# Image tokens: the second layernorm's scaling on GpSimd, the last image group in two parts

## The reference, cut to what matters

```
x = img.reshape(B, C, h, P, w, P)                       # 32 images, 14 x 14 patches of 16 x 16 x 3
x = jnp.transpose(x, (0, 2, 4, 3, 5, 1)).reshape(B, h * w, P * P * C)
x = _layernorm(x, ln1_g, ln1_b)                         # over 768 values
x = jnp.einsum('bnp,pd->bnd', x, W_proj) + b_proj       # to 192 values
x = _layernorm(x, ln2_g, ln2_b)                         # over 192 values: the second layernorm
x = jnp.concatenate([cls, x], axis=1) + pos_embedding
```

## Time and profile before

| | us |
|---|---|
| median of three runs | 1464.76 (1461.38 to 1465.84) |
| the profiled execution | 1464.05 |
| its span, first to last instruction | 1462.3 |
| PE busy | 1204.1 (82%) |
| DVE busy | 774.7 (53%) |
| ACT busy | 518.2 (35%) |
| POOL busy | 401.0 (27%) |
| image stage | from the start to about 244 |

### The profile page before, as it was taken

One profiled execution on the slowest core, in us unless ns is written; L12 is line 12 of the kernel. 1 busy time (PEld: TensorE's weight loads), 2 busy tenths in 40 slices (PEclk: granted clock), 3 DMA queues, 4 the chain that ended last, 5 costly groups with the idle time before them and its releaser, 6 DMA issues. The chain is left out here.

```text
span 1462.3 us, 32216 instructions
## 1 busy us (share of the span) xinstructions
PE 1204.1 (82%) x9176; PEld 1140.5 (78%) x9177; DVE 774.7 (53%) x2365; ACT 518.2 (35%) x1098; POOL 401.0 (27%) x358
## 2 busy tenths in 40 slices
PE   0498990268479999999999599973999999999996
PEld 0498890135369898898997499973999999999996
DVE  1578967874652633534436378772444444444442
ACT  0265651246562332233233266651222222222221
POOL 7270002800200301202103035552233333232332
PEclk9999995576589998998999799985999999999998
DMA  9754213022510423233233789941111111111110
GB/s 181 166 133 120 73 34 90 6 4 79 239 25 2 100 76 80 63 100 80 68 99 76 239 265 309 295 145 56 39 42 41 39 41 40 40 41 41 44 38 12
DMA packets 165144, 133.77 MB, mean 91 GB/s; under 512 B 79366, under 2 KB 154141, under 8 KB 163425
## 3 DMA queue, kind: packets, MB, share of 16 engines
q1 hardware_dynamic: 151264, 112.30, 28.8%
q0 software_dynamic: 10256, 17.41, 3.8%
q10 hardware_dynamic: 3538, 3.01, 0.8%
HBM read 89.97 MB, written 43.53 MB: 91 GB/s over the span
## 5 line engine op out<-in xcount | busy, mean ns | idle before, releaser
L2192 PE MATMUL ph<-zt,wc 96*128 96x128 f32 (+1 forms) x2136 | 258.2, 277 | 1.6 <-ACT zt L2107 1.6
L2192 PEld LDWEIGHTS ph<-zt,wc 96*128 96x128 f32 (+1 forms) x2136 | 254.9, 194 | 2.5 <-ACT zt L2107 2.5
L2095 POOL DMA_INDIRECT out_dram<-ob,oi x89 | 136.9, 1538 | 309.8 <-DVE ob L2139 309.8
L2113 ACT ACTIVATE ht<-ph 128x384 f32<-128x384 f32 x178 | 87.5, 492 | 325.2 <-PE ph L2192 325.2
L2180 PE MATMUL py<-w2e,ht 128*128 x1068 | 189.1, 327 | 0.8 <-DVE yb L2134 0.8
L1469 PE MATMUL pa<-wi,xn 96*85 (+3 forms) x2048 | 185.6, 246 | 2.9 <-POOL mc L1321 2.8
L1469 PEld LDWEIGHTS pa<-wi,xn 96*85 96x85 f32 (+1 forms) x2048 | 180.2, 155 | 4.2 <-POOL mc L1321 3.1
L2180 PEld LDWEIGHTS py<-w2e,ht 128*128 128x128 f32 x1068 | 172.1, 191 | 1.1 <-issue 1.0
L1332 POOL TENSOR_TENSOR bd<-rr,mc 128x656 f32<-128x656 f32 x48 | 61.5, 1282 | 307.1 <-PE pb L1487 187.5
L2134 DVE TENSOR_TENSOR yb<-py,b2e 128x192 f32<-128x192 f32 x89 | 31.8, 358 | 200.5 <-PE py L2180 200.5
L326 PE MATMUL ps_y<-wg,xt 128*112 128x192 f32 x672 | 123.3, 335 | 15.6 <-DVE yg L411 15.6
(11 more groups left out here) (310 smaller groups left out, 1844.3 us busy)
## 6 DMA issues: line engine op xcount, KB each, us to landing
y<-yd SPq DMA_DIRECT2D x41, 384.0 KB, 3.9
gp<-kd SPq DMA_DIRECT2D x48, 246.0 KB, 2.8
xg<-in_x SPq DMA_DIRECT2D x16, 588.0 KB
xr<-xs SPq DMA_DIRECT2D x89, 98.0 KB, 1.9
yd<-yt SPq DMA_DIRECT2D x56, 144.0 KB, 1.9
hb<-h SPq DMA_DIRECT2D x41, 192.0 KB, 4.3
yd<-yt SPq DMA_DIRECT2D x40, 192.0 KB, 2.1
xg<-in_x SPq DMA_DIRECT2D x48, 112.0 KB
```

The costliest lines, as they stand in the source:

```text
L2095: pool.indirect_dma_start(out, bass.IndirectOffsetOnAxis(ap=oi[j][:, 0:1], axis=0), ob[j][:], None, bounds_check=bound, oob_is_err=False). ...
L2113: act.activation(ht[j][:, 3 * k:3 * k + 3, :], ph[k][:], ACT.Gelu).then_inc(act_ok, 1)
L2192: m = pe.matmul(ph[k][:, c, :], wc[j][0:HD + d, d, f:f + 128], zt[j][0:HD + d, d, :], start=(d == 0), stop=(d == 1))
```

## The change: what it does

The two scaling operations leave DVE's loops. GpSimd gets, for pairs of columns, three operations per column instead of DVE's two: tensor_scalar (y - mean) * 1/std, tensor_tensor * gamma, tensor_tensor + position. GpSimd starts a group when DVE has done the reciprocal, which now raises `y_sqrt` itself. DVE keeps takes, statistics and moments, and waits for `y_scaled` before the statistics of scaled rows. The gathers of variable rows are issued in two batches of 16, behind GpSimd's groups 0 and 1. In the last group DVE computes moments for columns 0 to 7 (CUT = 8) after column 9, ACT takes their root after its copy of column 9, and GpSimd scales them from after column 11 on; the remaining six come after column 13, three (OWN = 3) scaled by GpSimd and three by DVE. SP stores the last group as columns 0 to 7 and 8 to 13.

```diff
@@ -150,6 +150,7 @@
         y_var = sem("y_var")
         y_sqrt = sem("y_sqrt")
         y_mid = sem("y_mid")
+        own = sem("y_own")
         y_scaled = sem("y_scaled")
         row_done = sem("row_done")
         tick = keep["tick"]
@@ -208,7 +209,7 @@
                                                    lo * PATCH:hi * PATCH],
                                          xv[g * GB + b][:, c, :, lo * PATCH:hi * PATCH]).then_inc(x_in[g % 2][n], 16)
             for g in range(NGRP):
-                for lo, hi in ((0, GRID),) if g + 1 < NGRP else ((0, GRID // 2), (GRID // 2, GRID)):
+                for lo, hi in ((0, GRID),) if g + 1 < NGRP else ((0, CUT), (CUT, GRID)):
                     sp.wait_ge(row_done, GRID * g + hi)
                     for b in BORDER:
                         row = (g * GB + b) * LP + 1
@@ -239,11 +240,40 @@
                 pool.indirect_dma_start(keep["tk"][:, b * 6:(b + 1) * 6], None, io["tok_tab"],
                                         bass.IndirectOffsetOnAxis(ap=keep["tid"][:, b:b + 1], axis=0)
                                         ).then_inc(gath, 16)
-            pool.wait_ge(tab, TAB_STORED)
-            for b in range(B):
-                pool.indirect_dma_start(keep["vr"][:, b * 70:(b + 1) * 70], None, dr["var_tab"],
-                                        bass.IndirectOffsetOnAxis(ap=keep["vid"][:, b:b + 1], axis=0)
-                                        ).then_inc(gath, 16)
+
+            def scale(g, cols):
+                for w in cols:
+                    r = yg[g % NY][:, w, 0:D]
+                    pool.tensor_scalar(r, r, muy[:, w:w + 1], rsy[:, w:w + 1], ALU.subtract, ALU.mult
+                                       ).then_inc(y_mid, 1)
+                for w in cols:
+                    r = yg[g % NY][:, w, 0:D]
+                    pool.wait_ge(y_mid, 2 * (GRID * g + cols[0]) + w - cols[0] + 1)
+                    pool.tensor_tensor(r, r, g2[:], ALU.mult).then_inc(y_mid, 1)
+                for w in cols:
+                    r = yg[g % NY][:, w, 0:D]
+                    pool.wait_ge(y_mid, 2 * (GRID * g + cols[0]) + len(cols) + w - cols[0] + 1)
+                    pool.tensor_tensor(r, r, pos[:, w, :], ALU.add).then_inc(y_scaled, 1)
+
+            def rows(lo, hi):
+                for b in range(lo, hi):
+                    pool.indirect_dma_start(keep["vr"][:, b * 70:(b + 1) * 70], None, dr["var_tab"],
+                                            bass.IndirectOffsetOnAxis(ap=keep["vid"][:, b:b + 1], axis=0)
+                                            ).then_inc(gath, 16)
+
+            for g in range(NGRP - 1):
+                pool.wait_ge(y_sqrt, 2 * g + 2)
+                for w in range(0, GRID, 2):
+                    scale(g, (w, w + 1))
+                if g == 0:
+                    pool.wait_ge(tab, TAB_STORED)
+                if g < 2:
+                    rows(g * B // 2, (g + 1) * B // 2)
+            pool.wait_ge(y_sqrt, 2 * NGRP)
+            for w in range(0, CUT, 2):
+                scale(NGRP - 1, (w, w + 1))
+            pool.wait_ge(y_sqrt, 2 * NGRP + 2)
+            scale(NGRP - 1, range(CUT, GRID - OWN))
             pool.wait_ge(gath, 16 * 2 * B)
 
         @block.scalar
@@ -276,9 +306,9 @@
                 act.copy(xt[j][:, 3:6, :], ps_t[j][1][:]).then_inc(turned_out, 1)
 
             act.sem_inc(projected, 2)
-            def root_y(g):
-                act.wait_ge(y_var, g + 1)
-                act.activation(rsy[:], vey[:], ACT.Sqrt).then_inc(y_sqrt, 1)
+            def root_y(n, lo=0, hi=GRID):
+                act.wait_ge(y_var, n + 1)
+                act.activation(rsy[:, lo:hi], vey[:, lo:hi], ACT.Sqrt).then_inc(y_sqrt, 1)
 
             def steps(g, lo, hi):
                 with act.Fori(lo, hi) as p:
@@ -294,7 +324,12 @@
                 steps(g, 0, EARLY)
                 if g:
                     root_y(g - 1)
-                steps(g, EARLY, GRID // 2 - 1)
+                if g + 1 < NGRP:
+                    steps(g, EARLY, GRID // 2 - 1)
+                else:
+                    steps(g, EARLY, CUT // 2 + 1)
+                    root_y(g, 0, CUT)
+                    steps(g, CUT // 2 + 1, GRID // 2 - 1)
                 for j in range(2):
                     take(g * GRID + GRID - 2 + j, j)
                     if g + 1 < NGRP:
@@ -302,7 +337,7 @@
                             root(g + 1)
                             act.wait_ge(x_rstd, g + 2)
                         normalise(g + 1, j, j)
-            root_y(NGRP - 1)
+            root_y(NGRP, CUT, GRID)
             act.wait_ge(misc, 1 + 16)
             act.wait_ge(cls_ok, 1)
             act.dma_start(h0.rearrange("(b t) d -> b t d", t=LP)[:, 0, :], cls_row[:]).then_inc(misc, 16)
@@ -388,16 +423,21 @@
                 dve.scalar_tensor_tensor(out=nb[g % 2][:], in0=mx[g % 2][:], scalar=-1.0, in1=rs[g % 2][:],
                                          op0=ALU.mult, op1=ALU.mult).then_inc(x_rstd, 1)
 
-            def y_moments(g):
-                link(dve.memset(dfy[:], 0.0))
-                dve.tensor_tensor(muy[:], sty[:, :, 1], sty[:, :, 4], ALU.add)
-                dve.tensor_tensor(vey[:], sty[:, :, 2], sty[:, :, 5], ALU.add)
-                link(dve.tensor_tensor(dfy[:], sty[:, :, 1], sty[:, :, 4], ALU.subtract))
-                dve.tensor_scalar(muy[:], muy[:], 0.5, None, ALU.mult)
-                dve.tensor_scalar(vey[:], vey[:], 1.0 / D, EPS, ALU.mult, ALU.add)
-                link(dve.tensor_tensor(dfy[:], dfy[:], dfy[:], ALU.mult))
-                dve.scalar_tensor_tensor(out=vey[:], in0=dfy[:], scalar=0.25, in1=vey[:], op0=ALU.mult, op1=ALU.add
+            def y_moments(lo=0, hi=GRID):
+                s, mu, df, v = sty[:, lo:hi, :], muy[:, lo:hi], dfy[:, lo:hi], vey[:, lo:hi]
+                link(dve.memset(df, 0.0))
+                dve.tensor_tensor(mu, s[:, :, 1], s[:, :, 4], ALU.add)
+                dve.tensor_tensor(v, s[:, :, 2], s[:, :, 5], ALU.add)
+                link(dve.tensor_tensor(df, s[:, :, 1], s[:, :, 4], ALU.subtract))
+                dve.tensor_scalar(mu, mu, 0.5, None, ALU.mult)
+                dve.tensor_scalar(v, v, 1.0 / D, EPS, ALU.mult, ALU.add)
+                link(dve.tensor_tensor(df, df, df, ALU.mult))
+                dve.scalar_tensor_tensor(out=v, in0=df, scalar=0.25, in1=v, op0=ALU.mult, op1=ALU.add
                                          ).then_inc(y_var, 1)
+
+            def y_scales(n, lo=0, hi=GRID):
+                dve.wait_ge(y_sqrt, 2 * n + 1)
+                dve.reciprocal(rsy[:, lo:hi], rsy[:, lo:hi]).then_inc(y_sqrt, 1)
 
             def col(t, w):
                 return t[:, bass.ds(w, 1), :].rearrange("r a d -> r (a d)")
@@ -416,18 +456,22 @@
                 dve.bn_stats(col(sty, w), y_col(g, w))
 
 
-            def scale_mul(g, w, n):
-                for a in range(n):
-                    r = y_col(g, w + a)
-                    dve.scalar_tensor_tensor(out=r, in0=r, scalar=muy[:, bass.ds(w + a, 1)], in1=g2[:],
-                                             op0=ALU.subtract, op1=ALU.mult).then_inc(y_mid, 1)
-
-            def scale_add(g, w, n):
-                for a in range(n):
-                    dve.wait_ge(y_mid, g * GRID + w + a + 1)
-                    r = y_col(g, w + a)
-                    dve.scalar_tensor_tensor(out=r, in0=r, scalar=rsy[:, bass.ds(w + a, 1)], in1=col(pos, w + a),
-                                             op0=ALU.mult, op1=ALU.add).then_inc(y_scaled, 1)
+            def scale_own(g, lo, hi):
+                for w in range(lo, hi):
+                    r = yg[g % NY][:, w, 0:D]
+                    dve.scalar_tensor_tensor(out=r, in0=r, scalar=muy[:, w:w + 1], in1=g2[:],
+                                             op0=ALU.subtract, op1=ALU.mult).then_inc(own, 1)
+                for w in range(lo, hi):
+                    r = yg[g % NY][:, w, 0:D]
+                    dve.wait_ge(own, w - lo + 1)
+                    dve.scalar_tensor_tensor(out=r, in0=r, scalar=rsy[:, w:w + 1], in1=pos[:, w, :],
+                                             op0=ALU.mult, op1=ALU.add).then_inc(own, 1)
+                for w in range(lo, hi):
+                    dve.wait_ge(own, hi - lo + w - lo + 1)
+                    dve.bn_stats(yg[g % NY][:, w, D:HR], r_of(g, w)).then_inc(row_done, 1)
+
+            def r_of(g, w):
+                return yg[g % NY][:, w, 0:D]
 
             def scale_stats(g, w, n):
                 dve.wait_ge(y_scaled, g * GRID + w + n)
@@ -443,8 +487,6 @@
                         y_take(g, 2 * p + j, j)
                         if more:
                             x_stats(g + 1, 2 * p + GRID - 2 * LATE + j)
-                        if scale:
-                            (scale_mul, scale_add)[j](g - 1, w, scale)
                         y_stat(g, 2 * p + j)
                     if scale:
                         scale_stats(g - 1, w, scale)
@@ -481,8 +523,7 @@
                     x_arrived(g + 1, 0)
```

(26 more changed lines are left out.)

## The result

The changed kernel took 1503.55 us (median of four, 1502.78 to 1504.22) against 1463.07 for the kernel before (four, 1459.14 to 1465.84) on the same chip: a ratio of 1.0279 [1.0251, 1.0306], slower by some 40 us. I had forecast 1466.5 and a range to 1478.

What follows compares the result with a forecast made beforehand. Image stage bound by SP's loads, then PE, then a serial tail of scaling and stores; its end shifts the rest. Store issue 244.5 against 242.3: 1464.05 + 2.2 = 1466.3, forecast 1466.5, range 1460.5 to 1478.

Steps and rivals of the forecast that it cites:

- 2 x 0.37: GpSimd's two tensor_scalars per pair of columns, each taken as 0.42 us long and started every 0.37 unlinked.
- P: GpSimd's time per pair of columns, two tensor_scalar and four tensor_tensor: forecast 4 x 0.49 + 2 x 0.37 = 2.70 us.
- Above, six linked operations of 0.58: Upper bound on P: GpSimd's six operations at 6 x 0.66 = 4.0 us; the lower bound was 1.7.
- (D): Rival: GpSimd operations take twice DVE's time, P = 3.9, +31 us (1495); chance 5%.
- The slope: From P = 2.75, each 0.1 costs 2.1 us in GpSimd's scaling chain and 0.4 in the last group's columns 0 to 7.
- my own sum: Image stage's store issue ends at 244.5 against 242.3, +2.2 us; above P = 2.75, 2.4 plus 25 times the excess.
- the slow projection: PE's projection of the last group's column 10, forecast to start at 212.0, its take at 214.25.
- the root held back by DVE's moments and holding PE: Last group: ScalarE's root, ahead of copy 10, waits for DVE's moments until 210.95; PE loses 5.1 us.
- the gathers' new place harmless for the block's end: Gathers behind groups 0 and 1 add 40.4 us to GpSimd's queue and end at 188, long before the block.
- rival (B): ScalarE's root does not hold PE up; columns 0 to 7 start 4.9 us earlier, -2.7 us at P = 2.7; chance 13%.
- Contention: DVE beside GpSimd: nothing added for takes and statistics; moments and DVE's own three columns collide, hidden except when GpSimd is idle.
- edge: P = 2.75, where GpSimd's 1.1 us of cover for scaling group 2 before DVE needs it at 208.15 ends.

Runs made afterwards that it cites:

- four kernels that differ in P alone: Changed kernel without tensor_scalar, with mult/add for subtract/mult, with constants for the pointers, and as written; ratios to the kernel before 1.0012, 1.0103, 1.0167, 1.0279.
- the one with all three repairs: Changed kernel with mult/add for subtract/mult, gathers ahead of the scaling, ScalarE's root behind copy 11: 1463.75 us against 1464.65 for the kernel before, ratio 1.0000.

## Why the prediction was wrong, step by step

**The step that failed is the price of the tensor_scalar**, the term "2 x 0.37" in P. I set it between a memset and a tensor_tensor, since it reads more than the one and less than the other. It took 1.00. The trace of before had no GpSimd tensor_scalar, and the order "more operands, more time" did not hold here: the form with one tensor and two scalars was twice the tensor_tensor. The pitch of the tensor_tensor was slightly off too, 0.52 for 0.49. Together: 4 x 0.52 + 2 x 1.00 = 4.08 against a measured 4.05, for my 2.70.

**The bound failed with it.** "Above, six linked operations of 0.58" gave 4.0 and was passed. It took a slow tensor_tensor for the longest operation possible (and its 0.58 stands in no row; my interpolation gave 0.54). A form without a row has no upper bound from the rows of another form. My chance for (D), 5%, at P = 3.9, came from the same confidence: its rule of twice DVE's time gave nearly the right P, for a reason that did not hold (the tensor_tensors are 1.6 times DVE's 0.33, the tensor_scalar three times).

**The slope was right.** "From there each 0.1 costs 2.1 us in its chain and 0.4 in part one": four kernels that differ in P alone have stages of 170.0, 179.2, 195.3 and 203.9 us at P = 2.06, 3.04, 3.72 and 4.05. By the slope the steps between them are 10.0 (3.9 in part one, 21 x 0.29 = 6.1 in the chain), 17.0 and 8.3; measured 9.2, 16.1 and 8.7. With P = 4.05 in my own sum the stage is 2.4 + 25 x 1.30 = 34.9 us longer; the measured 36.4 (38.3 less the 1.9 of the loads' later start) leaves 1.5.

**That rest is the slow projection**, which I had at its usual 2.1 us. In the changed kernel PE was idle for 14.85 us before it. PE's timeline and the window around it:

```profile
240.76 4.18 PE L361 MATMUL ps_y<-wg,xt 128*112 128x192 f32 x12 [14.85 <-ACT xt L306]
```

```profile
238.00:243.00 5.00, 2.24 (x7) 2.18 (x8) 1.58 (x11) 3.28 (x7) 0.00 (x0) 0.50 0.48 124
```

The granted clock was 0.50 from 238 to 243 us and 1.00 again from 247 to 251. From the end of the statistics to the start of part one I had 8.35 us (209.85 to 218.2); it took 9.98 (238.75 to 248.73), 1.6 more; the projection alone was 2.1 longer, and the steps around it a little shorter than I had put.

**Right as they stood,** the first two seen in the kernel without the tensor_scalar, since GpSimd was the bound in the changed one: the takes 2.53 apart up to column 9 and take 9 at 206.6 (206.22); the root held back by DVE's moments and holding PE (5.2 us for 5.1); the last eight stores directly behind the eight before (13.3 us for sixteen, forecast 13.2); the gathers' new place harmless for the block's end, though I counted their 40.4 us in GpSimd's chain and did not ask what the chain would be without them (14 us less at this P). One sum of rival (B) was off by itself: its part one starts at 206.6 + 5.06 + 0.96 + 0.35 = 213.0 and not at 213.3.

**Contention: right about the place, and paid where it was hidden.** Takes and statistics stayed at 0.36 us, the statistics at a pitch of 0.27. DVE's own three columns did collide: three scalar_tensor_tensors took 4.43 us, against 0.34 each in the earlier trace rows. One of the three took nearly all of it. The timeline of DVE and GpSimd from 267.65 to 271.1:

```profile
266.88 1.01 POOL L247 TENSOR_SCALAR yg<-yg,muy,rsy 112x192 f32<-112x192 f32 x1
...
267.51 3.75 DVE L462 SCALAR_TENSOR_TENSOR yg<-yg,muy,g 112x192 f32<-112x192 f32 x1
267.85 1.62 POOL L252 TENSOR_TENSOR yg<-yg,g 112x192 f32<-112x192 f32 x3
269.42 1.62 POOL L256 TENSOR_TENSOR yg<-yg,pos 112x192 f32<-112x192 f32 x3
```

It ended at 271.26, 0.2 us behind the last of GpSimd's six tensor_tensors (271.04). The one before it, wholly beside a tensor_scalar, took 0.43, and the one behind it 0.41. They lay beside part one's stores, as forecast. The Trainium skill ("SBUF — State Buffer", Who interferes with whom) gives this as an exclusive lock on a shared port pair, which whoever issues first holds for the whole instruction. The trace agrees only in part. The DVE operation did wait for whole tensor_tensors, but for six in a row, which all started after it; and beside GpSimd's tensor_scalar, which reads SBUF too, a DVE operation with two SBUF inputs was hardly held: 0.43 here, and 0.24, 0.15 and 0.15 for three small ones at 253.05 to 253.30.

## What to carry to other kernels

Price an operation that moves to another engine from a row of that engine, that operation and that shape; if there is none, the price has no upper bound, and the range has to hold a factor of two and more. When the receiving engine works in a serial chain, compute its edge first (here P = 2.75) and how many times the price is repeated above it (here 25), because that slope turned 0.6 us on one instruction, which a pair has twice, into 35 us. And before other work is left ahead of or between the new work in the same queue (the gathers, the root), ask who needs it then: the root cost 6 us (with the tensor_scalar gone) and the gathers 14 (at P = 4.05), and neither was needed where it stood.

## What the runs showed of the hardware that was not expected

- GpSimd's tensor_scalar at 112x192, half of a line of two: 1.00 us for subtract with mult or mult with subtract, 0.75 for one operation alone with a pointer, 0.49 for mult with add or add with mult, 0.34 for mult with add and constants.
- The part of a GpSimd tensor_scalar with two pointers that does not grow with its elements was about 0.33 us in both forms measured at two sizes. It is not one of every GpSimd operation: with two constants the whole of mult with add took 0.34, and a tensor_tensor of four elements 0.205 (two linked ones in 0.49).
- PE at the 1.2 GHz level (granted clock 0.50) behind pauses of 5.2 and 14.85 us: twelve matmuls in 4.17 and 4.18 us instead of 2.12.
- DVE's small operations on the moments wait beside GpSimd's tensor_tensors as its large ones on two SBUF tiles do; its bn_stats and its takes did not. DVE's timeline in the kernel without the tensor_scalar, then in the one with all three repairs, both beside GpSimd's scaling of part one:

```profile
225.63 0.62 DVE L426 TENSOR_TENSOR dfy<-sty 112x6 f32<-112x6 f32 x1
```

```profile
219.58 2.01 DVE L427 TENSOR_TENSOR muy<-sty 112x6 f32<-112x6 f32 x1
```

Such an operation on eight columns took 0.16 at 210.03 in the first of them, when GpSimd was idle. The 2.01 us lie beside four tensor_tensors that began at 219.46 and ended at 221.56; the next operation (L428), beside a tensor_scalar, took 0.16 again. No run of this study says why a wait spanned one tensor_tensor in the first kernel and four in the second.
